# Stacked score terms, wider down products and five smaller edits in a two-layer attention and MoE kernel

## The reference

```python
def _L0_xattn_ref(q, kv, mem, w_q, w_kv, w_concat):     # 16 heads of 16; one shared k and v
    c = jnp.concatenate([mem, kv], axis=1)               # mem and kv are the same 77 rows here
    qh = (q @ w_q).reshape(B, L, N_HEAD, D_HEAD).transpose(0, 2, 1, 3)
    k, v = (kvp[..., :D_HEAD], kvp[..., D_HEAD:])        # kvp = c @ w_kv
    attn_prob = jax.nn.softmax(jnp.einsum('bhid,bjd->bhij', qh, k) / np.sqrt(D_HEAD))
    ...
def _L0_ffn_ref(x, router_w, gate_w, up_w, down_w):      # 8 experts of 1024 hidden columns
    ...
        mean_w = jnp.where(cnt > 0, w_tok.sum() / jnp.maximum(cnt, 1.0), 0.0)
        h = jax.nn.silu(xf @ gw.T) * (xf @ uw.T)
        out = out + mask[:, None].astype(xf.dtype) * (h @ dw.T) * mean_w
```

## Time and profile before

| what | value |
| --- | --- |
| runs of the kernel before | 740.53, 743.98, 744.17 us; median 743.98 |
| profiled execution, own time | 745.15 us |
| its span, first to last instruction | 743.4 us |
| mean granted PE clock | 0.988 |
| busy: PE, DVE, ACT, POOL | 699.7, 560.6, 490.1, 337.4 us (94, 75, 66, 45% of the span) |
| chain that ended last | PE 70%, DVE 14%, POOL 5%, issue 4%, ACT 4%, DMA 2% |

### The profile page before, as it was taken

The page is one execution under the profiler, slowest core; times in us unless marked ns, Lnnn a source line. Parts: engine busy times, 40 slices in busy tenths (PEclk is TensorE's granted clock), DMA queues, the critical chain, the costliest instruction groups (busy, mean ns, idle before and its releaser), DMA issues.

```text
span 743.4 us, 14230 instructions
## 1 busy us (share of the span) xinstructions
PE 699.7 (94%) x4989; PEld 623.0 (84%) x4989; DVE 560.6 (75%) x992; ACT 490.1 (66%) x847; POOL 337.4 (45%) x333
## 2 busy tenths in 40 slices
PE   6899999989989999999999999999989879999994
PEld 6676777678989989998999899998978638999984
DVE  5776755686968868886868786886878978788847
ACT  3377777645647767776767676776746956787841
POOL 6558777502043323333233323332234657778840
PEclk9899999999999999999999999999999999999998
DMA  5000002267657868885877886795465264555439
GB/s 195 1 2 1 0 1 86 86 211 274 230 151 233 290 182 257 234 288 181 253 208 234 257 264 206 235 287 174 139 171 232 71 214 121 154 160 155 151 115 325
DMA packets 58264, 130.64 MB, mean 176 GB/s; under 512 B 6705, under 2 KB 30258, under 8 KB 58194
## 3 DMA queue, kind: packets, MB, share of 16 engines
q1 hardware_dynamic: 46674, 109.09, 43.1%
q0 software_dynamic: 11232, 20.46, 12.4%
q10 hardware_dynamic: 288, 0.19, 0.1%
HBM read 106.90 MB, written 22.81 MB: 174 GB/s over the span
## 4 chain that ended last, share of the span: by engine, by line
PE 70%; DVE 14%; POOL 5%; issue 4%; ACT 4%; DMA 2%; DVEq 0%; ACTq 0%; SPq 0%; POOLq 0%
PE ps L365 63%; DVE w_lo L1411 4%; POOL p_lo L749 2%; ACT w_hi L913 2%; PE ps L2570 2%; DVE h_lo L1411 1%; DVE x_all L2131 1%; PE ps L2806 1%; PE ps L2527 1%; DMA xm_d<-xnb 1%; PE ps L2279 1%; DVE hf L1853 1%; PE ps L2648 1%; DMA x_all<-in_x 1%; POOL xnb L862 1%
## 5 line engine op out<-in xcount | busy, mean ns | idle before, releaser
L1411 DVE TENSOR_TENSOR w_lo<-wr,w_hi 128x1024 fp32r<-128x1024 f32 x144 | 175.2, 1222 | 26.8 <-ACT w_hi L913 26.2
L804 POOL DMA_INDIRECT x_d<-ye,sca x39 | 74.1, 1900 | 247.6 <-ACT ye L1106 202.1
L913 ACT ACTIVATE w_hi<-wr 128x1024 fp32r<-128x1024 f32 x144 | 150.6, 1050 | 3.0 <-PE ps L365 2.2
L365 PE MATMUL ps<-xe_hi,w_lo 128*128 128x256 f32 x488 | 138.0, 283 | 0.0
L365 PE MATMUL ps<-xe_hi,w_hi 128*128 128x256 f32 x480 | 137.6, 287 | 0.2 <-DVE xe_lo L1411 0.2
L365 PE MATMUL ps<-xe_lo,w_hi 128*128 128x256 f32 x480 | 136.0, 283 | 0.0
L365 PE MATMUL ps<-w_hi,h_hi 128*128 128x256 f32 x312 | 91.7, 294 | 4.0 <-DVE h_lo L1411 2.2
L365 PEld LDWEIGHTS ps<-xe_hi,w_hi 128*128 128x128 f32 x480 | 92.2, 192 | 3.0 <-DVE xe_lo L1411 3.0
L365 PEld LDWEIGHTS ps<-xe_hi,w_lo 128*128 128x128 f32 x488 | 93.8, 192 | 0.1
L365 PEld LDWEIGHTS ps<-xe_lo,w_hi 128*128 128x128 f32 x480 | 92.2, 192 | 0.0
L365 PE MATMUL ps<-w_lo,h_hi 128*128 128x256 f32 x312 | 89.0, 285 | 0.0
(11 more groups left out here) (391 smaller groups left out, 1758.2 us busy)
## 6 DMA issues: line engine op xcount, KB each, us to landing
wr<-in_w SPq DMA_DIRECT2D x144, 512.0 KB, 4.5
dr<-in_w1d SPq DMA_DIRECT2D x24, 256.0 KB, 3.0
xn_d<-xnb SPq DMA_DIRECT2D x8, 512.0 KB, 3.7
raw<-in_w1gu SPq DMA_DIRECT2D x8, 512.0 KB, 9.2
x_d<-x_all SPq DMA_DIRECT2D x4, 512.0 KB, 4.6
x_all<-x_d SPq DMA_DIRECT2D x4, 512.0 KB, 4.3
xm_d<-xnb SPq DMA_DIRECT2D x4, 512.0 KB, 4.0
xnb<-y_d SPq DMA_DIRECT2D x4, 512.0 KB, 5.2
```

Source lines behind the costliest of these rows:

```text
L365: return nc.tensor.matmul(out, w, x, start=start, stop=stop, skip_group_check=True)
L804: pool.indirect_dma_start(dst, bass.IndirectOffsetOnAxis(ap=sca[n][:, col + half:col + half + 1], axis=0), ye[:, t % 2, half, :], None, co ...
L913: return s.activation(o, i, ACT.Copy)
L1411: return v.tensor_tensor(o, a, b, ALU.subtract)
```

## The change

1. **Scores.** For units 1 to 11 (40 of the 44 blocks) a block's three products of 102 rows become two: one of 96 rows that stacks the three terms of the block's two heads (`ks` x `qs`: k_hi, k_hi, k_lo against q_hi, q_lo, q_hi, 32 rows each), and one of 6 rows (96 to 101, the offsets). Blocks begin at `START` (0, 128, 231, 359) so that no block touches more than two heads; they have 128, 103, 128 and 103 rows (before 128, 128, 128 and 78). SP fills `ks` (12 transfers) and `qs` (a ring of 3 buffers; 3 transfers for each block, 120 in all, 32 partitions x 2 KB each).
2. **Unread products.** Four stand before the rows of group 1 are turned, three before the values of block 0.
3. **Means.** `sum_weights` and the part of the mean that needs no sum (`mean_tiles`) stand before tile 0, `mean_weights` at its end; tile 0's copy-out moves from tile 1 to the end of tile 0.
4. **Down products.** `w_hi` and `w_lo` become halves of one tensor `w_hl`; `down_row` makes hi x (hi | lo) as one product of 512 columns into both halves of the bank, and hi-weights x h_lo as before. The last tile is left as it was. DVE adds the two halves: `y_lo0`, one instruction of 256 columns per half tile (38 of them), after ACT's `y0`.
5. **Whole slots.** `place` sums slots straight into int32 and compares `iota_q` (bf16) with `sa_i`, `sb_i` (int32); the copies to `slot_i`, `sa_f`, `sb_f` go.
6. **Second attention.** The choice is made of 12 + 4 rows of 128; `top_of1(3)` and `statistics1(1)` stand before `keep_logits1(0)`, `exceed` after `keep_logits1(2)`; all of POOL's scalings wait for the same first choice.

```diff
-            cut = NT // 2 if r is r1 else NT - GT
+            cut = NT - GT
...
+            def stack_keys(j):
+                at = slice(START[j], START[j] + SIZE[j])
+                for k, part in enumerate((k_hi, k_hi, k_lo)):
+                    sp.dma_start(ks[k * PAIR:(k + 1) * PAIR, :, j, 0:SIZE[j]].bitcast(f32), part[pair_rows(j), :, at].bitcast(f32)).then_inc(w_in[5], 16)
+            def stack_queries(u):
+                sp.wait_ge(q_ls, parts_done(u))
...
+                if u > QRING:
+                    sp.wait_ge(s_mm, FIRST[u - QRING + 1])
+                for j in range(BLOCKS_OF[u]):
+                    for k, part in enumerate((q_hi, q_lo, q_hi)):
+                        sp.dma_start(qs[u % QRING][k * PAIR:(k + 1) * PAIR, j, :].bitcast(f32), part[pair_rows(j), slot_of(u), :].bitcast(f32)
+                                     ).then_inc(w_in[2 + u % QRING], 16)
...
+                if u >= 1:
+                    if j == 0:
+                        pe.wait_ge(w_in[2 + u % QRING], stacked(u))
+                    if b == FIRST[1]:
+                        pe.wait_ge(w_in[5], 16 * 3 * NW)
+                    mm(out, ks[:, bt, j, 0:w], qs[u % QRING][:, j, :], True, False)
+                    if j == 0:
+                        pe.wait_ge(mt_ok, u + 1)
+                    mm(out, k_hi[UK:UM, bt, cols], q_hi[UK:UM, slot_of(u), :], False, True).then_inc(s_mm, 1)
+                    return
...
+        def down_row(bank, hh, hl, wb, ws, start, stop):
+            mm(ps[:, bank, :].rearrange("p (k n) -> p k n", k=2), hh, w_hl[:, :, wb, ws], start, False)
+            return mm(ps[:, bank, 0:D], hl, w_hi[:, wb, ws], False, stop)
...
+            def y_lo0(t):
+                for half in range(SPAN[t]):
+                    dve.wait_ge(dn_ok, NU + halves(t, half))
+                    v.scalar_tensor_tensor(ye[:, t % 2, half, :], ps[:, 4 + half, D:2 * D], mw_t[:, SLOT[t]:SLOT[t] + 1],
+                                           ye[:, t % 2, half, :], ALU.mult, ALU.add).then_inc(f0["y_ok"], 1)
...
-                link(v.tensor_reduce(slot2[:, :, :], picked[:, :, :, :], AX.X, ALU.add))
-
-                link(v.tensor_copy(slot_i[:, :, :], slot2[:, :, :]))
...
-                v.tensor_copy(sb_f[:, :, :], sb_i[:, :, :])
-                link(v.tensor_copy(sa_f[:, :, :], sa_i[:, :, :]))
+                    ins = v.tensor_reduce(slot_i[:, :, :], picked[:, :, :, :], AX.X, ALU.add)
...
-                    ins = v.tensor_tensor(oh_a[:, c, :, :, :], places(COLS), turned_row(sa_f[:, c, :], COLS), ALU.is_equal)
+                    ins = v.tensor_tensor(oh_a[:, c, :, :, :], places(COLS), turned_row(sa_i[:, c, :], COLS), ALU.is_equal)
...
+                if g == 1:
+                    bank_free(pe, "x", KC + 1)
+                    idle_products(4, bank_of("x", KC + 1))
...
+                if b == 0:
+                    pe.wait_ge(q_ls, 4)
+                    idle_products(3, 3)
```

More of the change, by code:

```diff
@@ L21 @@
 NW = -(-UW // P)
+PAIR = 2 * DH
+KS = 3 * PAIR
+START = [NKEY * 3 * (j // 2) + P * (j % 2) for j in range(NW)]
+SIZE = [min(P, NKEY * (3 - j % 2) - P * (j % 2) + NKEY * (j % 2)) for j in range(NW)]
+HEAD = [3 * (j // 2) + j % 2 for j in range(NW)]
+assert SIZE == [128, 103, 128, 103]
+QRING = 3
 NU = NG * HG
@@ L189, in build_program @@
         sb_i = sb("sb_i", [P, 2, NT], i32)
-        sa_f = sb("sa_f", [P, 2, NT], bf16)
-        sb_f = sb("sb_f", [P, 2, NT], bf16)
         ex = picked[:, 0, :, :]
@@ L278, in build_program @@
         wr = sb("wr", [P, NB0, WB])
-        w_hi, w_lo = sb("w_hi", [P, NB0, WB], f32r), sb("w_lo", [P, NB0, WB], f32r)
+        w_hl = sb("w_hl", [P, 2, NB0, WB], f32r)
+        w_hi, w_lo = w_hl[:, 0, :, :], w_hl[:, 1, :, :]
         ws_hi, ws_lo = ws_hl[:, 0, :, :, :], ws_hl[:, 1, :, :, :]
@@ L413, in width, with pair_rows, stacked, loaded @@
         def width(u, j):
-            return min(P, HEADS_OF[u] * NKEY - P * j)
+            return min(SIZE[j], HEADS_OF[u] * NKEY - START[j])
+        def pair_rows(j):
+            return slice(HEAD[j] * DH, HEAD[j] * DH + PAIR)
+        def stacked(u):
+            return 16 * 3 * sum(BLOCKS_OF[i] for i in range(1, u + 1) if i % QRING == u % QRING)
+        def loaded(t, b):
+            first = {2: stacked(NU - 3), 3: stacked(NU - 2), 4: stacked(NU - 1), 5: 16 * 3 * NW}
+            return first.get(b, 0) + 16 * (t + 1)
         def group(t, g):
@@ L561, in _ @@
             sp.dma_start(bv[:, :], A["bv"]).then_inc(l1_in, 16)
+            def stack_keys(j):
[4 more added lines that the diff above has]
+                sp.wait_ge(q_ls, parts_done(u))
+                if u == 2 * HG - 1:
+                    sp.wait_ge(p_ls, 1)
+                if u > QRING:
[4 more added lines that the diff above has]
+                                     ).then_inc(w_in[2 + u % QRING], 16)
+            sp.wait_ge(kv_hi, 1)
+            sp.wait_ge(kv_lo, 1)
+            for j in range(NW):
+                stack_keys(j)
+            for u in range(1, NU):
+                stack_queries(u)
             with sp.Fori(0, NG) as g:
@@ L1089, in w0_hi @@
             def w0_hi(t, b):
-                act.wait_ge(w_in[b], 16 * (t + 1))
+                act.wait_ge(w_in[b], loaded(t, b))
                 copy(w_hi[:, b, :], wr[:, b, :]).then_inc(f0["w_hi"], 1)
@@ L1106, in y0 @@
                     s.activation(ye[:, t % 2, half, :], ps[:, 4 + half, 0:D], ACT.Copy,
-                                 scale=mw_t[:, SLOT[t]:SLOT[t] + 1]).then_inc(f0["y_ok"], 1)
+                                 scale=mw_t[:, SLOT[t]:SLOT[t] + 1]).then_inc(dn_ok, 1)
             def pair0(t):
@@ L1141, in pair0 @@
                     w0_hi(t + 1, 5)
+                if t == 0:
+                    y0(t)
             def single0(t):
@@ L1458, in _ @@
             v.memset(zpad[:, :], 0.0)
-            v.memset(vraw[:, :, NW - 1, 0:UK], 0.0)
+            for j in range(1, NW, 2):
+                v.memset(vraw[:, :, j, 0:UK], 0.0)
             dve.wait_ge(const_ok, 2)
@@ L2326, in scores @@
                     pe.wait_ge(p_ex, b - 1)
+                out, cols = ps[0:w, b % 2, :], slice(START[j], START[j] + w)
+                if u >= 1:
[8 more added lines that the diff above has]
+                    return
                 if j == 0:
@@ L2542, in down @@
                 q, j = k // 2 if row is None else row, k % 2
-                out, hs = ps[:, 4 + half, 0:D], slice(half * P, (half + 1) * P)
+                hs = slice(half * P, (half + 1) * P)
                 ws = slice((k % 4) * D, (k % 4 + 1) * D)
-                mm(out, h_hi[:, q, j, hs], w_hi[:, wb, ws], start, False)
-                mm(out, h_hi[:, q, j, hs], w_lo[:, wb, ws], False, False)
-                return mm(out, h_lo[:, q, j, hs], w_hi[:, wb, ws], False, stop)
+                return down_row(4 + half, h_hi[:, q, j, hs], h_lo[:, q, j, hs], wb, ws, start, stop)
             def gate_up0(t, q):
@@ L2578, in down_single @@
                     hh, hl = (h[:, part, :, :].rearrange("p c n -> p (c n)")[:, hs] for h in (h_hi, h_lo))
-                    mm(ps[:, 4, 0:D], hh, w_hi[:, G0 + part, ws], k == 0, False)
-                    mm(ps[:, 4, 0:D], hh, w_lo[:, G0 + part, ws], False, False)
-                    ins = mm(ps[:, 4, 0:D], hl, w_hi[:, G0 + part, ws], False, k == 7)
+                    if t < T0 - 1:
+                        ins = down_row(4, hh, hl, G0 + part, ws, k == 0, k == 7)
+                    else:
+                        mm(ps[:, 4, 0:D], hh, w_hi[:, G0 + part, ws], k == 0, False)
+                        mm(ps[:, 4, 0:D], hh, w_lo[:, G0 + part, ws], False, False)
+                        ins = mm(ps[:, 4, 0:D], hl, w_hi[:, G0 + part, ws], False, k == 7)
                 if part:
@@ L2589, in pair0 @@
                         down_single(t - 1, 1)
-                    if t == 1 and q == 1:
-                        pe.wait_ge(ws_ok, 1)
-                        mm(ps[:, 6, 0:E], ones[:, :], wsum[:, :], True, True).then_inc(ws_mm, 1)
+                if t == 0:
+                    pe.wait_ge(ws_ok, 1)
+                    mm(ps[:, 6, 0:E], ones[:, :], wsum[:, :], True, True).then_inc(ws_mm, 1)
                 if t == 1:
```

73 lines of the change are left out of this document (41 added, 32 removed).

## The result

| | median of the runs, us | runs | ratio to before | 95% interval |
| --- | --- | --- | --- | --- |
| before | 740.88 | 8 | | |
| changed | 747.63 | 8 | 1.0098 | 1.0068 to 1.0129 |

The changed kernel is 1.0% slower, some 7 us. Two of its eight executions were far longer than the rest, 757.29 and 760.11 us, and the last is left out of the ratio. The forecast was 742 with a range from 730 to 749: the time lies in the range, its sign and its likeliest case were wrong. The profiled execution of the changed kernel took 749.51 us with a span of 747.8.

What follows compares the result with a forecast made beforehand. PE was taken to bound the attention, with waits at the routers behind DVE and POOL. Terms +3.1 - 2.3 - 3.8 - 2.8 + 2.4 + 1.2 = -2.2 on 745.15 gave 742.9, less 1.2 to the median: 742, range 730 to 749.

Steps and rivals of the forecast that it cites:

- likeliest case: Whole kernel: the forecast's own case, 738 to 747 us, given 50%.
- Scores, +3.1: Attention, 40 blocks: one product of 0.233 saved, one stay in the small shape costing 0.31, so 3.1 us slower.
- the change is cheap: Attention scores: the shape change costs half a stay's price (735.6 us) or nothing (729.6); chance 25%.
- My slower rival: Attention scores: a stay costs 0.5, PE emptying and refilling at both changes, +10.7 instead of +3.1, 749.6 us; chance 13%.
- the lower bound: Attention scores: no cost for the stay in the small shape, so -9.3 us.
- the first rival: Attention scores: the shape change is cheap, 735.6 us at half a stay's price, 729.6 at nothing; chance 25%.
- Unread products, -2.3: Early attention, 35.28 to 39.93: seven products in gaps hold the clock, twelve products win 0.19 each, 2.3 us saved.
- Means, -3.8: First FFN, tile 1: with the mean ready, PE's waits of 0.31 and 1.87 and 1.6 of low clock go.
- Down products, -2.8: FFN down products: one of 512 columns replaces two of 256, 304 times, saving 2.8 us; DVE's additions cost 0.
- Whole slots, first router, +2.4: First router: int32 compares take 6.3 instead of 3.4 us, three small copies go (-0.5), nothing hides it: 2.4 us slower.
- Second router and order, +1.2: Second router: `place` starts 1.0 later, compares add 2.4, slack of 2.2 comes off: 1.2 us slower.
- the slack: Second router: DVE's last index was ready 2.56 before the gather, about 0.3 of it issue, leaving 2.2 us.

Runs made afterwards that it cites:

- `c_fullheight`: Changed kernel with the 6-row offsets' product made over all 102 rows, against a key tile with zeros in rows 0 to 95: 741.41 us, ratio 0.9987.
- `c_scores3`: Changed kernel with the three score products of before for all units and no stacking transfers: 743.57 us, ratio 1.0029.
- the control: The kernel before, unchanged, run and profiled a second time: 740.11 us, ratio 0.9986, span 737.8.
- `d_means`: Changed kernel with 16-bit slots and three score products (738.02 us), and the means computed where they were before: 743.99 us, ratio 1.0008.
- `c_slots16`: Changed kernel with the slots copied from int32 to 16-bit again before the compares: 741.82 us, ratio 1.0005.
- `d_order`: Changed kernel with 16-bit slots and three score products (738.02 us), and the second attention's order and 8 + 8 choice of before: 735.92 us, ratio 0.9905.

## Why the prediction was wrong

The sum was -2.2 us; the medians differ by +6.7. By its own steps:

- **Scores, +3.1.** Right in mechanism, and in size nearly. A stay costs 0.35 us, not 0.31: 0.09, 0.17 and 0.09 among products of 512 columns, against the 0.09, 0.16 and 0.07 that I had added up for one-row products. Undone, the part gives back 4.1. The rival "the change is cheap" (25%) is refuted: `c_fullheight`, where the change is gone, is 6.2 us faster. My slower rival had a stay of 0.5, because PE empties and refills; the weight loads show why there is a price at both changes, but it isn't 0.5, and that rival's time of 749.6 was near the measured one for other reasons. The premise that a product taken out is time taken out failed: of 9.3 us of products less, 2.2 came off (`c_fullheight` against `c_scores3`), so a free change of shape would not have been worth the 9.3 that the lower bound and the 729.6 of the first rival counted. The Trainium skill, TensorEngine Tiling (Array Packing), Key Properties, says that changing the tiling mode, and not just the tile, drains TensorE. The trace agrees, with 0.32, 0.42 and 0.32 instead of 0.233 each around a product of 6 rows.
- **Unread products, -2.3.** This failed. The stretch at 0.50 is in the changed kernel, two us later, and the control doesn't have it, whose group of executions is the larger one (76 of 107). I had priced a clock stretch from one execution that took 4 us longer than the median of the runs. Undone, the part costs 0.7, not told from 0.
- **Means, -3.8.** The wait is gone, which was right; by its own row it was 1.54 and not 1.87. The 1.6 of low clock behind it wasn't in the control. What the part is worth rose with the wide down products, whose additions would stand in the way of the old place (`d_means`, 6.0).
- **Down products, -2.8.** Right in sign: 1.0 to 2.2, and 1.8 in the traces. The additions are nearly hidden. Means and down products together are the 3.8 us that the first FFN is shorter than in the control, where 6.6 were forecast; that leaves some 2 for the means.
- **Whole slots, first router, +2.4.** Right: 12.4 us of compares against 6.8 in both routers, 2.2 us on the chain against the control and 2.5 against `c_slots16`. The Trainium skill, VectorE: DVE Perf Modes, What auto-detection actually checks, wants every tensor 16-bit for the doubled mode; the trace agrees with 1.2 against 0.63 ns a column.
- **Second router and order, +1.2.** This is the step that failed most. Against the control the changed profile loses 1.4 up to `cmp_b` and 4.9 behind it; by medians it is 2.1 for the order (`d_order`) and 3.3 for the slots (`c_slots16`), 5.4 together. The place of `place` was right, 1.4 later where I had 1.0. What was wrong is the slack: I had reasoned that 2.2 us before the gather would absorb what DVE loses. But the gather isn't what the second FFN waits for: PE waited 0.17 us for its rows in the kernel before, and not at all in the control and in the changed kernel. The product that waits for `ohb` is PE's, and behind it in PE's order stand the shared expert's groups, which have to be done before the second FFN begins. The longer wait, 5.6 us against 3.7, pushed all of them back, and the half clock behind it was longer too. I had named only DVE's side of the wait and POOL's, not the queue of the engine that waits.

By medians the misses are 4.2 us in this step, 2.8 in the first FFN, 1.6 in the unread products, 1.0 in the scores and 0.1 in the first router. That is 9.7, where the forecast missed by 8.9; each part is known to 1 or 2 us. Of the 8.9 us of gains that the sum had, 3.9 were clock, read from one execution. A chance of 0.16 for slower was too small for that. The time still fell into the range from 730 to 749 because that range is wide, and not because its terms were right.

## What to carry to other kernels

A small product among big ones is not small: leaving the array's full height and coming back cost 0.35 us here, one and a half products of 512 columns, and padding the operand with zero rows to the full height took that price away. When such a price is read from starts, both sides need the same neighbours: a tenth of a microsecond of the first reading belonged to the small turns in front. Before a clock stretch is counted as something to win, a second profile, or the distance of the profiled execution to the median of the runs, tells whether it is there as a rule. And when an operand comes later, the slack of the chain that was looked at isn't enough: what stands behind the waiting instruction in its own engine's order moves too, and may restart at half clock.
